# Q and K of each token tile: block transposes on VectorE and stores that put the blocks in place, instead of transposes on TensorE

## What is computed

```python
w = jax.nn.softmax(masked, axis=-1)            # [4096, 16], from the routing logits
def moe_proj(p):
    y = jnp.einsum('nc,ech->neh', x, p)        # p: [16, 256, 128]
    return jnp.einsum('ne,neh->nh', w, y)
q, k, v = moe_proj(q_proj), moe_proj(k_proj), moe_proj(v_proj)
scores = jnp.einsum('bth,bsh->bts', q, k) / jnp.sqrt(h)
o = jnp.einsum('bts,bsh->bth', softmax(scores), v)
out = jnp.einsum('enh,ehc->nc', jnp.einsum('ne,nh->enh', w, o), o_proj)
```

## Time and profile before

| | |
|---|---|
| median of 3 runs | 1463.84 us (1462.12 to 1465.78) |
| profiled execution | 1463.74 us, of which the profile's span is 1462.0 us |
| TensorE (PE) busy | 1381.4 us, 94% |
| weight loads (PEld) | 1212.9 us |
| VectorE (DVE) busy | 1152.2 us, 79% |
| ScalarE (ACT) / GpSimd (POOL) busy | 679.0 / 714.0 us |
| mean granted TensorE clock | 0.973 of full |

### The profile page before, as it was taken

The page is one execution under the profiler, slowest core; times in us unless marked ns, Lnnn a source line. Parts: engine busy times, 40 slices in busy tenths (PEclk is TensorE's granted clock), DMA queues, the critical chain, the costliest instruction groups (busy, mean ns, idle before and its releaser), DMA issues. The chain is left out here.

```text
span 1462.0 us, 20853 instructions
## 1 busy us (share of the span) xinstructions
PE 1381.4 (94%) x6880; PEld 1212.9 (83%) x6880; DVE 1152.2 (79%) x2185; ACT 679.0 (46%) x1345; POOL 714.0 (49%) x633
## 2 busy tenths in 40 slices
PE   5578999999999999999999899999999999999997
PEld 3458989999999999999999777878787878878775
DVE  5758586785876868767667688989999999999865
ACT  3340221302213022130001189888888888888983
POOL 3221131301313113121014167888888898989897
PEclk8688999999999999999999989999999999999998
DMA  4230110011100111000126440010100000000000
GB/s 136 71 97 15 31 38 27 26 39 30 38 27 26 38 30 38 27 26 24 52 84 204 134 152 15 8 37 9 37 8 22 24 15 29 15 30 15 15 15 22
DMA packets 84668, 63.24 MB, mean 43 GB/s; under 512 B 15520, under 2 KB 77392, under 8 KB 84304
## 3 DMA queue, kind: packets, MB, share of 16 engines
q1 hardware_dynamic: 56656, 46.69, 10.2%
q10 hardware_dynamic: 27904, 15.21, 3.6%
HBM read 36.72 MB, written 25.17 MB: 42 GB/s over the span
## 5 line engine op out<-in xcount | busy, mean ns | idle before, releaser
L1425 PE MATMUL ps<-w_hi,memory_r 128*128 128x384 f32 x2048 | 568.0, 343 | 5.8 <-DVE w_lo L858 2.8
L1217 DVE SCALAR_TENSOR_TENSOR wst<-ps,w_cur,wst 128x384 f32<-128x384 f32 x480 | 294.8, 614 | 175.0 <-PE ps L1425 163.6
L1425 PEld LDWEIGHTS ps<-w_hi,memory_r 128*128 128x128 f32 x2048 | 376.0, 189 | 9.9 <-DVE w_lo L858 2.9
L1643 POOL TENSOR_TENSOR memory_rest<-memory_rest,pf 128x512 f32<-128x512 f32 x248 | 346.5, 1397 | 65.9 <-ACT pf L1745 57.5
L1425 PE MATMUL ps<-w_lo,memory_r 128*128 128x384 f32 x1024 | 344.4, 336 | 0.0
L1810 DVE TENSOR_TENSOR p_lo<-pf,p_hi 128x512 fp32r<-128x512 f32 x256 | 282.4, 1103 | 38.3 <-ACT p_hi L1747 37.1
L1425 PEld LDWEIGHTS ps<-w_lo,memory_r 128*128 128x128 f32 x1024 | 194.0, 189 | 4.7 <-issue 1.4
L1745 ACT ACTIVATE pf<-ps 128x512 f32<-128x512 f32 x256 | 153.2, 598 | 70.4 <-PE ps L1917 63.4
L1705 ACT COPY ps<-shift_rows 128x512 f32<-128x512 f32 x256 | 152.8, 597 | 5.9
L1747 ACT ACTIVATE p_hi<-ps 128x512 fp32r<-128x512 f32 x256 | 152.0, 594 | 0.0
L1792 DVE TENSOR_REDUCE mx<-ps 128x1 f32<-128x512 f32 x224 | 147.5, 678 | 1.2 <-PE ps L1908 1.2
(11 more groups left out here) (213 smaller groups left out, 2112.4 us busy)
## 6 DMA issues: line engine op xcount, KB each, us to landing
qk_scratch<-wst ACTq DMA_DIRECT2D x56, 128.0 KB, 2.2
memory<-in_x SPq DMA_DIRECT2D x8, 512.0 KB, 4.1
x_scratch<-memory SPq DMA_DIRECT2D x8, 512.0 KB, 2.9
o_scratch<-memory_rest SPq DMA_DIRECT2D x16, 256.0 KB, 3.0
x2b<-x_scratch SPq DMA_DIRECT2D x32, 128.0 KB, 2.2
out_x<-memory_rest SPq DMA_DIRECT2D x32, 128.0 KB, 1.7
v_scratch<-wst ACTq DMA_DIRECT2D x60, 64.0 KB, 1.8
memory_r<-qk_scratch SPq DMA_DIRECT2D x9, 256.0 KB, 4.4
```

Source lines behind the costliest of these rows:

```text
L1217: nc.vector.scalar_tensor_tensor(out=dst, in0=src, scalar=w, in1=dst, op0=ALU.mult, op1=ALU.add).then_inc(moe_acc, 1)
L1425: ins = nc.tensor.matmul(ps[:, s % MOE_BANKS, 0:H3], x_part[p][:, k, rows], w_part[:, k, e].rearrange("p t h -> p (t h)"), start=(k == 0 a ...
L1643: nc.gpsimd.tensor_tensor(p_sum[:, p], p_sum[:, p], pf[:, j % PB], ALU.add).then_inc(p_summed, 1)
```

## The change

VectorE's 32x32 block transpose takes the Q and K columns of the accumulator, at step 1 of the next tile, and writes them to `qk_st[:, :, 1]` (`turn_qk`). In each block of 32 tokens by 32 head columns, rows and columns are then exchanged, but the blocks stand where they stood. ScalarE makes the high part of them, `qk_st[:, :, 0]`, now from SBUF; VectorE's `low_qk` subtracts it in place, both inputs now in SBUF. The stores put the blocks in their places: four per tile, one for each 32 tokens, each with 32 partitions of 16 runs of 32 tokens (128 B) in `qk_scratch`, whose layout becomes (P, 2, 2, N). `turn_qk` waits until the stores of the previous tile have landed (`qk_out`), since it overwrites their source. The TensorE transposes are kept for slot 7's own tiles. Some semaphores that are used once are folded into others; their waits are the same.

```diff
@@ scalar: high_parts, store_parts
-                    act.wait_ge(qk_mm, upto(i, p, TT, t + 1))
-                    wait(act, qk_out, upto(i, p, 32 * TT, 32 * t))
-                    nc.scalar.copy(qk_st[:, 0].bitcast(F32R),
-                                   ps[:, QK_BANK, 0:2 * P].rearrange("p (a n) -> p a n", a=2)).then_inc(qk_ready, 1)
+                    act.wait_ge(qk_turned, upto(i, p, TT, t + 1))
+                    nc.scalar.copy(qk_st[:, :, 0].bitcast(F32R), qk_st[:, :, 1]).then_inc(qk_ready, 1)
...
-                    for l in range(2):
-                        act.dma_start(qk_dram[l, :, :, cols], qk_st[:, l]).then_inc(qk_out, 16)
+                    first = (2 * i + p) * BT + t * P
+                    for a in range(QUADS):
+                        act.dma_start(qk_dram[:, :, :, first + a * QUAD:first + (a + 1) * QUAD].rearrange(
+                            "(b r) m l n -> r (m l) b n", r=QUAD),
+                                      qk_st[a * QUAD:(a + 1) * QUAD].rearrange("r m l (b n) -> r (m l) b n", n=QUAD)
+                                      ).then_inc(qk_out, 16)
@@ vector
+                def turn_qk(i, p, t):
+
+                    dve.wait_ge(moe_acc, upto(i, p, STEPS, (t + 1) * E))
+                    wait(dve, qk_out, qk_stored((2 * i + p) * TT + t))
+                    nc.vector.transpose(qk_st[:, :, 1], acc[:, t % 2, 0:2 * H].rearrange("p (m n) -> p m n", m=2)
+                                        ).then_inc(qk_turned, 1)
+
                 def low_qk(i, p, t):
...
-                        tt(qk_st[:, 1].bitcast(F32R), ps[:, QK_BANK, 0:2 * P].rearrange("p (a n) -> p a n", a=2),
-                           qk_st[:, 0], ALU.subtract).then_inc(qk_lo_ready, 1)
+                        tt(qk_st[:, :, 1].bitcast(F32R), qk_st[:, :, 1], qk_st[:, :, 0], ALU.subtract
+                           ).then_inc(qk_lo_ready, 1)
...
+                        if s == TURN_AT and 2 * i + p:
+                            turn_qk(*before(i, p), TT - 1)
+                        if e == TURN_AT and t and ahead:
+                            turn_qk(i, p, t - 1)
@@ tensor
-                        if s == 4 and not (isinstance(i, int) and 2 * i + p == 0):
-                            qk_transposes(*before(i, p), TT - 1)
-                        if e == 4 and t:
+                        if e == 4 and t and not ahead:
                             qk_transposes(i, p, t - 1)
```

More of the change, by code:

```diff
@@ L308, in adaln_block_kernel @@
         moe_acc = sem("moe_acc")
+        qk_turned = sem("qk_turned")
         qk_mm = sem("qk_mm")
@@ L335, in adaln_block_kernel @@
         N_PARAMS = 10
+        ZEROED, ONES, IDENT = 1, 2, 3
+        C_SIG, WIN_HI, CM_HI = 1, 2, 3
         MAX_FROM, MAX_EARLY = 8, TT * (KG - 1)
@@ L339, in adaln_block_kernel, with qk_stored @@
         OP_GROUPS = ((0, 3), (3, 6), (6, 8), (8, 8))
+        QUADS, QUAD = 4, P // 4
+        TURN_AT = 1
+        def qk_stored(tile):
+            return 16 * QUADS * min(tile, NT - TT) + 32 * max(tile - (NT - TT), 0)
         W_STAGE = [e % 3 if e < E - 4 else e % 2 for e in range(E)]
@@ L395, in _ @@
                 assert len(params) == N_PARAMS
-                sp.wait_ge(zeroed, 1)
+                sp.wait_ge(pool_const, ZEROED)
                 for dst, src in params:
@@ L640, in _ @@
                 act.wait_ge(cond_in, 16)
-                nc.scalar.activation(c_sig[:], c_col[:], ACT.Sigmoid).then_inc(sig_ready, 1)
+                nc.scalar.activation(c_sig[:], c_col[:], ACT.Sigmoid).then_inc(act_const, 1)
                 act.wait_ge(win_in, 16)
-                nc.scalar.copy(win_hi, win).then_inc(win_hi_ready, 1)
+                nc.scalar.copy(win_hi, win).then_inc(act_const, 1)
                 act.wait_ge(mod_mm, 2)
@@ L650, in _ @@
                 nc.scalar.activation(sig_gates[:], sig_gates[:], ACT.Sigmoid)
-                act.wait_ge(zeroed, 1)
-                nc.scalar.copy(cm_parts[0:3 * S, :], cm_ld).then_inc(cm_hi_ready, 1)
+                act.wait_ge(pool_const, ZEROED)
+                nc.scalar.copy(cm_parts[0:3 * S, :], cm_ld).then_inc(act_const, 1)
                 def split_w(e0, e1):
@@ L770, in last_tile @@
                     tile, cols = NT - TT + t, slice(N - BT + t * P, N - BT + (t + 1) * P)
-                    act.wait_ge(qk_mm, tile + 1)
+                    act.wait_ge(qk_mm, t + 1)
                     ins = nc.scalar.copy(k_hi[:, cols], ps[:, QK_BANK, P:2 * P])
@@ L774, in last_tile @@
                         ins.then_inc(k_hi_ready, 1)
-                    act.wait_ge(qk_out, 32 * tile)
+                    act.wait_ge(qk_out, qk_stored(tile))
                     nc.scalar.copy(qk_st[:, 0, 0].bitcast(F32R), ps[:, QK_BANK, 0:P]).then_inc(qk_ready, 1)
@@ L1078, in piece @@
                         route_piece(n, *c)
+                def turn_qk(i, p, t):
[3 more added lines that the diff above has]
+                                        ).then_inc(qk_turned, 1)
                 def low_qk(i, p, t):
                     dve.wait_ge(qk_ready, upto(i, p, TT, t + 1))
-                    wait(dve, qk_out, upto(i, p, 32 * TT, 32 * t))
                     if isinstance(i, int) and 2 * i + p == NB - 1:
@@ L1086, in low_qk @@
                         tt(k_lo[:, cols], ps[:, QK_BANK, P:2 * P], k_hi[:, cols].bitcast(F32), ALU.subtract)
-                        tt(qk_st[:, 1, 0].bitcast(F32R), ps[:, QK_BANK, 0:P], qk_st[:, 0, 0], ALU.subtract
+                        dve.wait_ge(qk_out, qk_stored(NT - TT + t))
+                        tt(qk_st[:, 0, 1].bitcast(F32R), ps[:, QK_BANK, 0:P], qk_st[:, 0, 0], ALU.subtract
                            ).then_inc(qk_lo_ready, 1)
                     else:
-                        tt(qk_st[:, 1].bitcast(F32R), ps[:, QK_BANK, 0:2 * P].rearrange("p (a n) -> p a n", a=2),
-                           qk_st[:, 0], ALU.subtract).then_inc(qk_lo_ready, 1)
+                        tt(qk_st[:, :, 1].bitcast(F32R), qk_st[:, :, 1], qk_st[:, :, 0], ALU.subtract
+                           ).then_inc(qk_lo_ready, 1)
                 def max_piece(n):
@@ L1171, in _ @@
                     norm_piece(n, 0, 1)
-                dve.wait_ge(cm_hi_ready, 1)
+                dve.wait_ge(act_const, CM_HI)
                 third = slice(2 * S, 3 * S)
@@ L1211, in slot @@
                         if e == 0:
-                            wait(dve, qk_mm, upto(i, p, TT, t - 1))
+                            wait(dve, qk_turned, min(upto(i, p, TT, t - 1), NT - TT))
+                            wait(dve, qk_mm, t - 1 if not ahead else 0)
                             wait(dve, v_split, upto(i, p, TT, t - 1))
@@ L1366, in qk_transposes @@
                     pe.wait_ge(moe_acc, upto(i, p, STEPS, (t + 1) * E))
-                    wait(pe, qk_lo_ready, upto(i, p, TT, t))
+                    pe.wait_ge(qk_lo_ready, upto(i, p, TT, t))
                     nc.tensor.transpose(ps[:, QK_BANK, 0:P], acc[:, t % 2, 0:H], ident[:])
@@ L1728, in start @@
                     seed(1)
-                    act.wait_ge(qk_out, 32 * NT)
+                    act.wait_ge(qk_out, qk_stored(NT))
                 def body(i, p, first, last):
```

35 lines of the change are left out of this document (16 added, 19 removed).

## The result

The changed kernel takes **1476.19 us** (median of 4 runs, 1473.45 to 1477.13), the kernel before beside it 1463.89 us. The ratio is 1.0085, 95% interval 1.0073 to 1.0097: 12.3 us slower. The profiled execution took 1473.45 us with a span of 1471.7 us; that is 9.7 us more than the profiled execution of before, and 2.7 us less than the median of its own kernel.

The account below looks back on a forecast made before the run. TensorE, busy nearly all the time in the mixture-of-experts stage, was taken as the bound. Against 1463.74 us, -6.3 + 9.3 + 1.3 + 0.6 + 3.0 = +7.9 us gave 1471.7 us, range 1461 to 1480.

Parts of the forecast that it names:

- rival 1: At step 22, low_qk comes between two POOL instructions and isn't held; only store issue costs: +4.9, 1468.7 us; chance 0.22.
- What is removed: TensorE in the experts: 28 of 32 transpose pairs go, 0.226 us each, -6.3 us.
- The logits: TensorE waits there for ScalarE's x_parts behind tile 1's stores: 1.3 us in six slots, 1.5 in slot 6, +9.3 us.
- X: What tile 1's stores take longer to issue on ScalarE's queue than before; taken as 1.5 us.
- The bound that went by the number of runs: ScalarE's queue: if issue time followed run count, a store of 512 runs takes 1.0 us, four 4.1; X = 2.8.
- 8X formula: Whole change as a function of X: 8X - 7.1 us, and 3.0 more if POOL holds low_qk.
- The K load: Last slot: the third K load is issued later behind ScalarE's stores and o_proj's chain, TensorE waits X - 0.2, +1.3 us.
- h2: Slot 6: VectorE's added transpose delays its second piece of h2, and the pair at step 36 saves nothing: +0.6 us.
- The block transpose: VectorE, step 1 of the next tile: 0.41 us by the nearest row, 0.35 net, hidden except in slot 6.
- Rival 5: VectorE's block transpose takes 1 us or more, costing at step 49 and slot 6: +3 us, 1475; 0.10 together with rival 4.
- rival 4: Short-run stores land late, VectorE's transpose waits for them: +10 us more, 1482; chance 0.10 together with Rival 5.
- The hold of low_qk: Step 22, slots 1 to 5: POOL's low_hidden holds low_qk, TensorE's out projection stands 0.6 us each, +3.0 us.

Follow-up runs that it names:

- four_stores: The kernel before with its two Q/K stores per tile cut into four of 64 partitions, still 512 B runs, transposes kept on TensorE: 1482.05 us.
- late_last: Changed kernel with tile 1's stores behind x_parts and the sigmoid, and slot 6's tile 3 stores behind slot 7's first high_o: 1457.38 us.
- n = 1 to 4: The kernel before with 1, 2, 3 or 4 chained, unread copies on ScalarE ahead of x_parts: 1464.97, 1466.71, 1477.82, 1483.34 us.

## Why the prediction was right, and where not

Forecast 1471.7 us, range 1461 to 1480, slower by over 0.3% with 0.60. It came out at 1476.2, inside the range, on the likelier side. The sum was +7.9 us; the medians differ by 12.3, the profiled executions by 9.7. That the number is near is in part luck. The terms that the prediction rightly had come to -6.3 + 8.6 + 1.8 + 0.7 = +4.8, 1468.7 us, which is rival 1's number and only 0.5 us on the slower side of its 0.3% line. Another 3.0 us that it had did not come, and some 6 to 8 us that it did not have did.

**What is removed: right.** 0.23 to 0.24 us a pair. The kernel with the pairs put back confirms the size, once its out-projection waits are taken off.

**The logits: right in place, mechanism and size.** X was taken as 1.5 and is 1.43; +9.3 was forecast, +8.6 measured. The choice to price a store by the row of a back-to-back store (0.64 us) and not by its runs was the good one: they take 0.65. The bound that went by the number of runs, 1.0 us a store, is refuted by these 0.65 us for 512 runs, and four_stores' 0.63 for 128 shows that the runs hardly count. The 8X formula held in its places. With X = 1.43 it gives 1.23 us for six of the slots, 1.43 for slot 6 and 1.23 for the K load; they took 0.90 to 1.39, 1.83 and 1.8, together 10.4 where it says 10.0. Putting the stores behind x_parts removes seven of its eight terms, and late_last the eighth.

**The K load and h2: right,** 1.8 for 1.3 and 0.7 for 0.6. late_last shows that the first hung on ScalarE's order and not on the DMAs. For h2 no run takes the block transpose away at that place; there only the step and the trace agree.

**The block transpose: 0.43 us** where 0.41 was the near row and 0.35 net were taken. It brought no wait elsewhere. Rival 5 falls, and so does rival 4: stores of 128 B runs land 2.2 us after their issue, as those of 512 B did, and VectorE never waited for them.

**The hold of low_qk: wrong, 3.0 us that didn't come.** The step that failed is "POOL's next instruction waits for nothing and is at hand when the V part ends". It is at hand, but 0.11 us too late: low_qk started on VectorE while the V part still ran. Rival 1 had the outcome right, though low_qk does not come between the two POOL instructions but over the end of the first. The price was right: with the order forced, five waits of 0.7 us, where 0.6 was worked out. The prediction named the 0.06 us between the arrivals as what was open, and that was so.

**The missing term.** Nothing in the sum, in a rival or in the signs let TensorE's clock answer to a wait. The step that failed is the one from stand to time: each stand was priced at its own length, and at the logits four of seven cost 1.57 us more. In the changed kernel's profiled execution that is 4 x 1.57 = 6.3 us. It took the place of the 3.0 of the hold and more: -6.3 + 8.6 + 1.8 + 0.7 + 6.3 - 0.3 = +10.8 for the stage, which with the start and the attention gives the 9.7 of the profiled executions within 0.1. The other executions of the changed kernel are 2.7 us longer, and their mean granted clock is 0.966 to 0.967, not 0.969. About two stretches more would make that; they were not profiled, so this is an estimate. The trace of before could have given the size. Behind stands of TensorE of 2.0 and 0.9 us, in the first steps of slot 0, it has a stretch of the same length and level (the window's row):

```profile
123.09:126.50 3.41, 3.41 (x13) 3.41 (x12) 1.41 (x5) 0.00 (x0) 0.00 (x0) 0.50 0.00 0
```

What it could not have given is which of the new stands would be followed by one: TensorE stands 0.86 us near 414 and 1.3 near 184 in it, and no stretch follows. But it had a rival in it: that the clock falls behind the new stands.

By its signs: "3.1 us of issue" (3.08), "logits stand over 1 us" (in six of seven slots; 0.9 in slot 0) and "steps 0.23 shorter" came true. "low_qk takes about 2.7 us" did not.

## What to carry to other kernels

A wait of the bound engine can cost more than its length: in this kernel 24 of 32 stands of 0.6 us and more at the logits were followed by 3.4 us at half the clock, 1.6 us each, and none of ten stands of 0.7 and 1.0 us at the out projection. So look at the windows' granted clock behind every new wait, since busy time doesn't show it.

DMAs issued from a compute engine's queue are paid by whatever stands behind them, some 0.65 us each for the three shapes measured here. Put them behind the work that another engine waits for: moving one line turned 0.85% slower into 0.3% faster.

Where a forecast hangs on which of two engines comes first by a tenth of a microsecond, give both orders a real chance: here a removed 0.23 us pair on a third engine decided it.

## What the runs showed that I had not expected

- A half-clock stretch of 3.41 us behind stands of TensorE at the logits. By the idle time before the weight loads there, 24 of 32 stands of 0.59 us or more were followed by one: in the changed kernel 4 of 7, with four stores 6 of 7, for n = 1 to 4 1 of 1, 0 of 1, 6 of 7 and 6 of 7, and with the logits one step later 1 of 2. None of the 11 stands of 0.15 to 0.44 us was, nor any of the fifteen of 0.50, 0.74 and 1.08 at the out projection. Of seven of 1.1 to 2.1 at the third K load one was.
- A VectorE subtraction with two SBUF inputs that starts 0.11 us ahead of a POOL instruction makes that one longer, 2.59 us instead of 2.39; started 0.13 us behind it, it is itself held, 2.54 instead of 0.43. Both in five slots of five.
- Four times as many runs of a quarter of the length, at 64 KB a store, cost ScalarE's queue only 0.02 us more per store (0.65 against 0.63), and nothing in landing (2.2 us).
